# Block 1 of a four-block network: attention scores go to their layout by token and head by way of a tensor in device memory

## The reference

```python
q, k = l2norm(q), l2norm(k)                                # 16 heads
dots = einsum('bhid,bhjd->bhij', q, k) * 10
dots = einsum('hg,bgij->bhij', W_pre_th, dots)             # mix over heads
dots = where(causal, -max, dots)
vk = top_k(dots, 64)[..., -1:]
attn = softmax(where(dots < vk, -max, dots))
attn = einsum('hg,bgij->bhij', W_post_th, attn)            # mix over heads
out = einsum('bhij,bhjd->bhid', attn, v) * head_scale
out = out * sigmoid(x @ Wg + bg) @ Wo
```

## Time and profile before

| | |
|---|---|
| median of 3 runs | 3859.69 us (3850.48 to 3867.26) |
| the profiled execution | 3863.54 us, its span 3862.2 us |
| PE, DVE, ACT, POOL busy | 91%, 88%, 80%, 45% of the span |
| DMA moved | 106.01 MB in 168124 packets |
| issues at L1264 | 1024 |

### The profile page before, as it was taken

The page is one execution under the profiler, slowest core; times in us unless marked ns, Lnnn a source line. Parts: engine busy times, 40 slices in busy tenths (PEclk is TensorE's granted clock), DMA queues, the critical chain, the costliest instruction groups (busy, mean ns, idle before and its releaser), DMA issues.

```text
span 3862.2 us, 78954 instructions
## 1 busy us (share of the span) xinstructions
PE 3518.2 (91%) x19551; PEld 2607.6 (68%) x19551; DVE 3405.6 (88%) x18541; ACT 3078.7 (80%) x10773; POOL 1751.2 (45%) x3672
## 2 busy tenths in 40 slices
PE   4999999996799999999999999999999999999987
PEld 3888888873566666666666666666666666666665
DVE  6888888853999999999999999999999999999994
ACT  5777777755788888888888888888888888888864
POOL 0000000002556556565656555656666665665553
PEclk7999999996899999999999999999999999999999
DMA  3000000001111111111111111111111111111110
GB/s 125 12 12 9 12 12 12 10 6 35 26 28 28 29 32 28 28 32 34 33 30 28 28 29 28 28 28 30 31 28 29 34 33 33 28 28 29 26 26 4
DMA packets 168124, 106.01 MB, mean 27 GB/s; under 512 B 78000, under 2 KB 165104, under 8 KB 166896
## 3 DMA queue, kind: packets, MB, share of 16 engines
q1 hardware_dynamic: 167664, 100.96, 12.2%
HBM read 20.70 MB, written 8.91 MB: 8 GB/s over the span
## 4 chain that ended last, share of the span: by engine, by line
PE 32%; DVE 25%; ACT 16%; SPq 10%; DMA 8%; issue 7%; POOL 2%; DVEq 0%; ACTq 0%; POOLq 0%
SPq L1264 9%; DVE W L1736 8%; DMA T<-SN 8%; PE bank L362 6%; DVE last L1757 6%; ACT SN L1529 5%; PE bank L1336 4%; PE bank L1321 3%; PE bank L1413 3%; ACT T L1516 3%; PE bank L330 3%; PE bank L194 3%; PE bank L1348 2%; DVE y L895 2%; ACT L1485 2%
## 5 line engine op out<-in xcount | busy, mean ns | idle before, releaser
L1736 DVE MATCH_REPLACE8 W<-last,W 128x130 f32<-128x130 f32 (+17 forms) x3456 | 889.9, 269 | 0.0
L1757 DVE MAX8 last<-W 128x8 f32<-128x130 f32 (+17 forms) x3456 | 780.0, 271 | 0.0
L1842 POOL TENSOR_SCALAR posts<-post,share 128x128 f32<-128x128 f32 x1024 | 368.2, 378 | 372.7 <-DVE share L1666 372.7
L1336 PE MATMUL bank<-T,pre 128*128 128x40 f32 (+15 forms) x1024 | 402.8, 477 | 107.3 <-DMA T<-SN 79.1
L885 DVE TENSOR_TENSOR_SCAN hs<-dA,dx 128x256 f32<-128x256 f32 x512 | 353.2, 690 | 133.9 <-issue 100.5
L1516 ACT ACTIVATE T<-T,peak 128x260 f32<-128x260 f32 (+15 forms) x1024 | 416.7, 435 | 30.1 <-POOL T L1893 28.2
L1529 ACT ACTIVATE SN<-bank,rq 128x260 f32<-128x260 f32 (+1 forms) x1024 | 361.1, 433 | 88.0 <-DMA T<-SN 43.8
L1893 POOL TENSOR_TENSOR T<-T,below 128x520 f32<-128x520 f32 (+12 forms) x416 | 360.6, 883 | 23.1 <-DVE below L1766 7.6
L1336 PEld LDWEIGHTS bank<-T,pre 128*128 128x128 f32 x1024 | 173.4, 199 | 278.1 <-ACT T L1537 119.1
L1348 PEld LDWEIGHTS bank<-posts,T 128*128 128x128 f32 (+7 forms) x2048 | 267.9, 185 | 110.3 <-issue 54.7
L1348 PE MATMUL bank<-posts,T 128*128 128x128 f32 (+7 forms) x2048 | 324.4, 298 | 18.7 <-POOL posts L1842 17.2
(11 more groups left out here) (244 smaller groups left out, 9611.2 us busy)
## 6 DMA issues: line engine op xcount, KB each, us to landing
T<-SN SPq DMA_DIRECT2D x32, 130.0 KB
x_in<-in_xT SPq DMA_DIRECT2D x32, 128.0 KB, 2.2
x_mid<-x_b SPq DMA_DIRECT2D x32, 128.0 KB, 1.7
xb<-x_mid SPq DMA_DIRECT2D x32, 128.0 KB, 2.1
out_y<-x_d SPq DMA_DIRECT2D x32, 128.0 KB, 3.4
T<-SN SPq DMA_DIRECT2D x32, 126.0 KB
T<-SN SPq DMA_DIRECT2D x32, 122.0 KB
T<-SN SPq DMA_DIRECT2D x32, 118.0 KB
```

Of the source, the lines that this page charges most:

```text
L1336: pe.matmul(MIX[:, 0:pair.shape[-1]], pre[:], pair, start=True, stop=True).then_inc(premixed, 1)
L1736: dve.match_replace(both[:, s, at:to], best[n], both[:, s, at:to], LOWEST).then_inc(ranked, 1)
L1757: dve.max(best[n], both[:, s, at:to]).then_inc(ranked, 1)
L1842: pool.tensor_scalar(posts[(4 * k + j) % NP][:], post[:], share[k % 2][:, j:j + 1], 1.0, ALU.mult, ALU.mult).then_inc(posts_made, 1)
```

## The change

The scores of a block are first stored from `SN` into a tensor in device memory, `by_token[blk]`, laid out as `SN` is (query, head, key), in pieces of 6, 6 and 4 heads (block 0) and of 6, 4, 4 and 2 heads (block 1). `STAGES` has, for each piece, its heads and the number of pieces of `s_kept` that it waits for. Then T is filled from that tensor, one DMA for a pair of groups (256 rows, always `width(g)` keys), and two for the pair (30, 31): 8 + 9 = 17 reads. `regroup` waits for all stored pieces of its block. ACT's `s_keep` now waits for the stored pieces of block 0 before it overwrites their heads, and, from the second sequence on, for the stored pieces of block 1 before the next block 0. `stage` waits until the reads of the sequence before have landed. PE waits for the same quarters, which count 32 (48 in the one with the pair (30, 31)). The beats are as they were.

```diff
+STAGES = [[(0, 6, 2), (6, 12, 4), (12, 16, 6)], [(0, 6, 6), (6, 10, 10), (10, 14, 14), (14, 16, 16)]]
...
+    by_token = [nc.dram_tensor(f"scores_by_token{blk}", [P, HEADS, KEYS], F32).ap() for blk in range(2)]
...
+    staged = [sems.sems(f"staged{blk}_", len(STAGES[blk])) for blk in range(2)]
...
+    def arrivals(blk, k):
+        return 32 + 16 * any(side(g) for g in PREMIX[blk][4 * k:4 * k + 4:2])
...
+        def stage(b, blk):
+            if b:
+                for k, sent in enumerate(regrouped[blk]):
+                    sp.wait_ge(sent, arrivals(blk, k) * b)
+            w = W_LO if blk == 0 else W_HI
+            for n, (lo, hi, pieces) in enumerate(STAGES[blk]):
+                sp.wait_ge(s_kept, S_ALL * b + S_BEFORE[blk] + pieces)
+                sp.dma_start(by_token[blk][:, lo:hi, 0:w], SN[:, lo:hi, 0:w]).then_inc(staged[blk][n], 16)
+
         def regroup(b, blk):
-            sp.wait_ge(s_kept, S_ALL * b + S_BEFORE[blk] + len(S_PIECES[blk]))
...
-            for k, g in enumerate(PREMIX[blk]):
+            for sent in staged[blk]:
+                sp.wait_ge(sent, 16 * (b + 1))
+            for k in range(HALF // 2):
+                g = PREMIX[blk][2 * k]
                 q = (g - blk * HALF) * QG
-                sp.dma_start(scores(b, g, 0, seen_by(g)), SN[q:q + QG, :, 0:seen_by(g)]).then_inc(regrouped[blk][k // 4], 16)
+                rows = by_token[blk][q:q + 2 * QG].rearrange("(two t) h n -> (t h) two n", two=2)
+                if side(g):
+                    for one in range(2):
+                        n = seen_by(g + one)
+                        sp.dma_start(scores(b, g + one, 0, n), rows[:, one, 0:n]).then_inc(regrouped[blk][k // 2], 16)
+                else:
+                    sp.dma_start(side_by_side(b, g), rows[:, :, 0:width(g)]).then_inc(regrouped[blk][k // 2], 16)
...
             if seq(f):
+                stage(f, 0)
                 regroup(f, 0)
+                stage(f, 1)
                 regroup(f, 1)
...
-                pe.wait_ge(regrouped[blk][k // 2], 64 * (b + 1))
+                pe.wait_ge(regrouped[blk][k // 2], arrivals(blk, k // 2) * (b + 1))
...
-            if blk == 1 and piece == 0:
-                for sent in regrouped[0]:
-                    act.wait_ge(sent, 64 * (b + 1))
+            for c, (lo, hi, pieces) in enumerate(STAGES[0]):
+                if blk == 1 and piece == lo:
+                    act.wait_ge(staged[0][c], 16 * (b + 1))
+            if b and n == 0:
+                for sent in staged[1]:
+                    act.wait_ge(sent, 16 * b)
```

## The result

The changed kernel takes 3724.53 us (median of 4 runs, 3722.32 to 3726.57), the kernel before 3855.09 beside it: a ratio of 0.9658, 95% interval 0.963 to 0.9685. That is 131 us less; forecast were 95 less, 3765 us, and the range ended at 3730. The direction and the place of the gain were right; its size was not, and it was the term for the clock that was too small.

A forecast was written before the change was run, and what follows sets the result against it. PE and DVE, both nearly full, were taken as the bound, held up by block 1's late T. (2.2 + 0.6) x 32 = 90 us and 6 at the start gave 96 us off: 3765 us, range 3730 to 3862.

The forecast's parts named there:

- The bound and the place: PE and DVE nearly full, held up by the score regrouping; T late for block 1 alone, 9.0 us after its last scores.
- Block 1's way: From block 1's last scores to T: T lands at 2098.1 instead of 2100.3, removing 2.2 of PE's 2.5 us idle.
- The clock: PE's matmuls after block 1's stall run partly at 1.2 GHz: between nothing and 1.1 us a sequence recoverable, 0.6 taken.
- The start, 6 us: In the first sequence ACT can begin block 1 some 6 us earlier, counted once.
- ACT's wait, nothing in the steady state: ACT's 43.8 us of waiting to overwrite SN goes; its 1.2 us in the steady state counts nothing, hidden by PE.
- Does DVE follow?: Whether DVE can shorten its period by 2.8 us, out of 4.8 us idle for mask and `share`: it fits, just.
- Block 0's way: Block 0's T through device memory arrives at 2068.4, before PE wants it at 2069.5: cost nothing, cover one microsecond at most.
- rival D: A new wait at block 0's first premix, store and read together over 6.0 us: slower, 3905 us; chance 0.11.
- trips that are 2 us longer: An estimate from the Trainium skill of 2 us more on each device memory trip, making both blocks late.
- Rival B: Hand-written orders fit the old arrival, so only about 1.2 us a sequence is gained: 3815 us; chance 0.13.
- C: The two device memory trips eat the gain, block 1's T only 0.5 us earlier: 3844 up to 3862 us; chance 0.12.
- rival A: The gain as summed from stall, clock and start: 3735 to 3822 us; chance 0.64.

The follow-up runs named there:

- block 1 alone: The changed kernel with block 0 regrouped from SN by sixteen DMAs as before, only block 1 going through device memory: 3728.76 us, ratio 0.9664.
- the filler: The kernel before with two more 128x512 matmuls of weights ahead of PE's wait for block 1's T: 3801.03 us, ratio 0.9855.
- one delay: The changed kernel with one more store, waited for, between the stored pieces and the reads of block 1: 3793.02 us, ratio 0.9836.

## Why the prediction was wrong

*The bound and the place* were right. The 9.0 us of block 1's way, PE's idle and DVE's behind it made the period; with block 1 alone nearly all of the gain is there, and with its arrival set back all of it is lost.

*Block 1's way, 2.2 of 2.5 us.* The way came out shorter, 6.0 us for 6.8: the store was confirmed 0.5 us sooner and two reads were issued in 0.84 us and not in 1.3, while the read took 3.0 us for 2.7. The term itself had the right size: (79.1 - 8.4)/32 = 2.2 us a sequence.

*The clock, "I take half, 0.6 us".* This is the step that failed. PE's busy time fell by 54.3 us, 1.7 a sequence, and the filler in the kernel before gives 1.6 to 1.7 in time. The term was too small twice. Its upper bound, 1.1 us, counted the eight matmuls of L1348 and the four of L1352 and left out the premix itself, which the clock slows too. This row of the same timeline before was not in the sum:

```profile
2102.16 1.53 PE L1336 MATMUL bank<-T,pre 128*128 128x488 f32 x2 [0.69 <-ACT T L1537]
```

The same two matmuls take 1.08 us in the changed kernel (2044.54 above), so with 0.45 for them, 0.8 and 0.3 this one period loses 1.6 us; the V pieces take 1.98 us in both and lose nothing. Over the whole span L1336 is busy 402.8 us before and 374.8 after, half of what PE saves. Then the bound was halved, and no row spoke for that. The difference is 1.1 us x 32 = 35 us, which is what the forecast gain of 96 us lacked of the measured 131; the forecast time was 5 us further off because the kernel before came out at 3855.09 and not at 3859.7.

*The start, 6 us* and *ACT's wait, nothing in the steady state*: right in the changed kernel (31.1 us of wait cost nothing beside block 1 alone). In a kernel that still has the stall, block 0's half is worth up to 0.9 us a sequence, perhaps by this wait.

*Does DVE follow?* It did, further than counted. 2.8 us of its 4.8 us were to go; a sequence became 4.4 us shorter. Its busy time is unchanged, its waits for the mask and for `share` fell by 86.5 and 54.5 us, together the 141 us by which the spans differ. The mask's wait in the steady state is 0.4 us, where the prediction left about 1. The 1.9 us at `share` hung on PE matmuls at the low clock, so they went with it; the filler took away the same 55 us with T as late as ever.

*Block 0's way.* Costed at nothing with a cover of one microsecond at most. PE waits for T nine times in all. The one wait of 3.7 us is block 0's, in the first sequence; the others, at most 0.6 us in the steady state, are all block 1's. So block 0's cover held and rival D did not come, nor did trips that are 2 us longer: the last store of block 0 (264 KB) landed after 2.6 us, where 2.1 were counted. It was close all the same: in the period from 2004 to 2090 the eight reads of block 0 start at 2011.95, the first two take some 2.0 us to land, and PE begins its 128x40 premix at 2014.49. Rival B (the hand-made orders cut the gain) and C (the trips eat it) did not come; one piece instead of four goes beyond C and is slower than the kernel before.

*The range.* Its low end had 3.6 us a sequence and the start, and so took the clock at 1.1. It is given as 3735 where rival A is summed and as 3730 where the range is; neither would have held 3724.53. With 2.2 for the stall, 1.7 for the clock and the start the sum is 3.9 x 32 + 6 = 131 us, which is what the medians differ by. That it fits so closely is in part luck: the two measured terms come from the profiled executions, and these differ by 141 us, as the one before was 8.4 us above its median and the one after 2.2 below. The further 10 us are the balance of PE's other waits, which no step named.

## What to carry to other kernels

Price a stall of TensorE twice: its own length, and all the matmuls behind it that run at the lower clock; here that nearly doubled each microsecond, and filling the idle with two dead matmuls gave back 1.45%. A regrouping from 8 partitions kept the sixteen DMA engines 0.43 busy while the queue was full, so a detour by way of device memory can be the shorter way, if it leaves in pieces while the data are made: in one piece it was slower than what it replaced. An engine that is busy 99% of a period is not yet a reason to unload it: ask first who waits for the result.

## What was not expected of the hardware

The last store of 260 KB and three reads of 126, 130 and 244 KB through device memory took 6.0 us with their issues, where four direct transfers of 496 KB in all took 9.0. An issue took 0.63 us with 8 partitions at its source, 0.40 to 0.50 for a read of 128 rows or more into 128 partitions. PE's clock fell after an idle of 2.53 us (0.72 in the 6 us behind it), and with one delay, 2.1 us of idle a sequence, its mean over 1300:3400 was 0.98.
